# A vision block on one core: values per token tile through DRAM, masked key eviction, new attention banks, q/k/v products nine tiles late, ternary rounding on POOL

## What is computed

```python
x = patches(img)                       # 64 x 36 x 768
x = layernorm(x, ln1_g, ln1_b) @ W + bias
x = layernorm(x, ln2_g, ln2_b) + pe
h = concatenate(cls_token + cls_pos_embedding, x)          # 64 x 37 x 256
q, k, v = split_heads(layernorm(h) @ Wqkv + bqkv)          # 16 heads of 16
q, k = q * cos + rotate_half(q) * sin, k * cos + rotate_half(k) * sin
h = h + (softmax(q @ k.T / 4) @ v) @ Wout + bout
y = layernorm(h)
h = h + bitlinear(gelu(bitlinear(y, W1, b1)), W2, b2)      # weights rounded to -1, 0, 1 times mean |W|
```

## Time and profile before

| what | us |
| --- | --- |
| median of three runs | 387.02 (383.44 to 388.23) |
| the profiled execution | 389.49 |
| its span, first to last instruction | 387.7 |
| TensorE busy | 328.3 (85%) |
| VectorE busy | 276.0 (71%) |
| ScalarE busy | 219.3 (57%) |
| POOL busy | 160.4 (41%) |

### The profile page before, as it was taken

One profiled execution on the slowest core, in us unless ns is written; L12 is line 12 of the kernel. 1 busy time (PEld: TensorE's weight loads), 2 busy tenths in 40 slices (PEclk: granted clock), 3 DMA queues, 4 the chain that ended last, 5 costly groups with the idle time before them and its releaser, 6 DMA issues.

```text
span 387.7 us, 9782 instructions
## 1 busy us (share of the span) xinstructions
PE 328.3 (85%) x3548; PEld 255.5 (66%) x3548; DVE 276.0 (71%) x680; ACT 219.3 (57%) x398; POOL 160.4 (41%) x329
## 2 busy tenths in 40 slices
PE   0648999999999957699889898989886789999874
PEld 0436777777777632588778787878774467777553
DVE  1184577686776675447776767677766899999983
ACT  2344455545577312244555555555553799999993
POOL 4223265464654525324332333323204556656630
PEclk9996999999999997657999999999999999999997
DMA  8997050000000000000000000000000000100101
GB/s 225 311 399 225 9 210 1 2 2 2 0 2 1 0 2 0 2 1 3 2 0 0 0 0 0 0 0 0 0 2 1 1 2 27 43 27 30 43 28 61
DMA packets 9018, 16.10 MB, mean 42 GB/s; under 512 B 944, under 2 KB 5744, under 8 KB 8992
## 3 DMA queue, kind: packets, MB, share of 16 engines
q1 hardware_dynamic: 7936, 13.59, 10.3%
q10 hardware_dynamic: 1056, 2.18, 2.2%
HBM read 13.34 MB, written 2.42 MB: 41 GB/s over the span
## 4 chain that ended last, share of the span: by engine, by line
PE 54%; DVE 18%; ACT 12%; issue 9%; DMA 3%; POOL 3%; ACTq 0%; DVEq 0%; POOLq 0%
PE ps L331 13%; PE ps L407 9%; PE ps L357 7%; DVE sc L811 6%; PE ps L439 4%; DVE ximg L830 4%; PE ps L321 3%; DMA qkT<-in_W 3%; PE ps L415 3%; ACT ximg L1023 2%; PE ps L426 2%; ACT ximg L976 2%; PE ps L314 2%; PE ps L365 2%; PE ps L401 2%
## 5 line engine op out<-in xcount | busy, mean ns | idle before, releaser
L1057 POOL TENSOR_TENSOR rs<-rs,nhalf 128x1 f32<-128x1 f32 (+1 forms) x76 | 41.8, 557 | 120.4 <-DVE rs L622 50.8
L962 ACT ACTIVATE ximg<-ps,byp 128x222 f32<-128x222 f32 x64 | 25.0, 442 | 61.0 <-PE ps L447 54.0
L331 PE MATMUL ps<-w_in,xT 128*128 128x256 f32 (+1 forms) x228 | 55.3, 394 | 2.9 <-ACT xT L896 2.9
L331 PEld LDWEIGHTS ps<-w_in,xT 128*128 128x128 f32 (+1 forms) x228 | 42.8, 195 | 10.5 <-ACT xT L896 4.2
L407 PE MATMUL ps<-hnT,w_v 128*128 (+1 forms) x256 | 38.9, 300 | 12.7 <-ACT ximg L976 7.6
L1101 POOL TENSOR_TENSOR ximg<-qkT,ones_c 128x148 f32<-128x148 f32 x32 | 15.9, 497 | 80.7 <-PE ps L401 79.5
L407 PEld LDWEIGHTS ps<-hnT,w_v 128*128 128x128 f32 x256 | 34.2, 208 | 18.1 <-issue 16.9
L756 DVE TENSOR_TENSOR ximg<-ps,tab 111x512 f32<-111x512 f32 x32 | 22.1, 691 | 31.9 <-PE ps L426 31.9
L357 PE MATMUL ps<-w_qk,hnT 128*128 128x512 f32 (+1 forms) x76 | 37.9, 623 | 6.7 <-DVE qb L673 6.7
L896 ACT ACTIVATE xT<-ps 128x768 f32<-128x768 f32 (+1 forms) x19 | 15.1, 794 | 32.0 <-PE ps L321 32.0
L665 DVE TENSOR_TENSOR qa<-ps,tab 128x512 f32<-128x512 f32 (+1 forms) x19 | 13.1, 689 | 27.8 <-PE ps L314 27.8
(11 more groups left out here) (107 smaller groups left out, 770.5 us busy)
## 6 DMA issues: line engine op xcount, KB each, us to landing
ximg<-in_x SPq DMA_DIRECT2D x18, 384.0 KB, 15.8
out<-ximg SPq DMA_DIRECT2D x18, 128.0 KB, 1.7
ximg<-in_W SPq DMA_DIRECT2D x2, 1024.0 KB, 6.3
wide<-in_rows ACTq DMA_DIRECT2D x1, 768.0 KB, 15.1
w_qk<-in_Wqk SPq DMA_DIRECT2D x1, 512.0 KB, 15.0
qkT<-in_offsets ACTq DMA_DIRECT2D x1, 448.0 KB, 13.3
qkT<-in_W SPq DMA_DIRECT2D x1, 384.0 KB, 6.3
qkT<-in_W ACTq DMA_DIRECT2D x1, 384.0 KB, 11.3
```

Source lines behind the costliest of these rows:

```text
L331: pe.matmul(dst[0:n, :], xT[t % 2][:, k, 0:n], w_in[:, k, :], start=(k == 0), stop=False)
L962: ins = act.activation(vds[u][:, m, :, :].rearrange("p i (r t) -> p i r t", r=3), src, ACT.Identity, bias=b_v[:, m:m + 1])
L1057: pool.tensor_tensor(rs[u][0:n, i:i + 1], rs[u][0:n, i:i + 1], nhalf[0:n, :], ALU.pow).then_inc(S[done], 1)
```

## The change

1. The q/k product of a tile is done nine steps behind its pixels instead of four (`LAG = 9`), with VectorE's rotation, POOL's add and the transposes moved with it. `hnT` becomes a ring of seven tiles. The patch stage is 30 steps long on TensorE instead of 25.
2. A values product per token tile (`value_product`, two products of 256 columns) follows each q/k product. ScalarE evicts it by head parity with a column of ones per head, SP stores it in DRAM (`vsc`), and two loads a pair, 48 rows x 2 images x 544 bytes each, bring it back in block form; four buffers `vb`, cleared by POOL, take them. The per-pair values product, its eviction, its four transposes and VectorE's placing are gone.
3. The keys are evicted twice, each with a parity mask as scale, so `scores` reads `qkT` directly and POOL's staging is gone.
4. Probabilities are padded to 64 columns a head and turned two heads at a time, four transposes in each of banks 4 and 5; `attend` is 16 products of 34 columns (32 records) into banks 6 and 7 by turns; the output is turned into the ends of banks 4 and 5. The attention loop is written out.
5. The values' bias goes through Wo into the output's offset row (`out_offset`), which needs Wo at the start; Wo and Wv are loaded after pixel tiles 2 and 3.
6. The six ternary passes go to POOL, after its last patch step; the two absolute sums of ScalarE go to steps 10 and 12, the total and the scales to steps 15 and 16.

```diff
+LAG = 9
+HB = LAG - 2
...
+            sp.dma_start(w_o[:], a["Wo"].rearrange("(k p) n -> p k n", p=128)).then_inc(S["ld_o"], 16)
+            load_x(3)
+            sp.dma_start(w_v[:], a["Wv"].rearrange("(k p) n -> p k n", p=128)).then_inc(S["ld_v"], 16)
...
+            def load_values(p):
+
+                if p < 4:
+                    sp.wait_ge(S["v_zero"], p + 1)
+                else:
+                    sp.wait_ge(S["o_ready"], p - 3)
+                for e in range(2):
+                    src = bass.AP(vsc.tensor, PW * p * VROW + e * HC * VW,
+                                  [[VROW, 48], [TOK * VROW, 2], [1, HC * VW]])
+                    sp.dma_start(vb[p % 4][64 * e:64 * e + 48, :, e, :], src).then_inc(S[f"vb{p % 4}"], 16)
...
+            for t in range(NT):
+                store_values(t)
+            sp.wait_ge(S["v_stored0"], 16 * (NT // 2))
+            sp.wait_ge(S["v_stored1"], 16 * (NT // 2))
+            for p in range(4):
+                load_values(p)
+            store_values(NT)
+            sp.wait_ge(S["v_stored0"], 16 * (NT // 2 + 1))
+            for p in range(4, NP):
+                load_values(p)
...
             def patch_step(s):
                 if live(s - 2, NT + 1):
                     position_rows(s - 2)
-                if live(s - 6, NT + 1):
-                    turn_qk(s - 6)
+                if live(s - LAG - 2, NT + 1):
+                    turn_qk(s - LAG - 2)
...
-                if live(s - 4, NT + 1):
-                    qk_product(s - 4)
+                if live(s - LAG, NT + 1):
+                    qk_product(s - LAG)
+                    value_product(s - LAG)
                 if live(s - 3, NT + 1):
                     turn_h(s - 3)
+                if s == 0:
+                    out_offset()
...
+            def turn_out(p, b):
+
+                pe.wait_ge(S["o_norm"], p + 1)
+                pe.wait_ge(S[f"p_evac{b}"], min(p + 2, NP))
+                war(pe, "o_canvas4" if b == 4 else "o_canvas", p, 1)
+                m = b - 4
+                pe.transpose(ps[:, b, O_AT:O_AT + SPAN], at[p % 4][0:SPAN, 128 * m:128 * m + 128],
+                             ident[0:SPAN, 0:SPAN]).then_inc(S[f"o_turned{b}"], 1)
...
+            def attention_step(s):
+                if live(s, NP):
+                    scores(s)
+                if live(s - 3, NP):
+                    turn_out(s - 3, 5)
+                    turn_out(s - 3, 4)
+                if live(s - 2, NP):
+                    attend(s - 2)
                 if live(s - 1, NP):
+                    turn_probs(s - 1, 4)
+                    turn_probs(s - 1, 5)
...
+            pe.wait_ge(S["y_mid"], NT + 1)
+            attention_step(0)
+            patch_step(NT + LAG + 1)
+            pe.wait_ge(S["h_ready"], NT + 1)
+            pe.wait_ge(S["v_evac"], NT + 1)
+            attention_step(1)
+            patch_step(NT + LAG + 2)
             pe.wait_ge(S["a_init"], 2)
+            for s in range(2, NP + 1):
+                attention_step(s)
...
+            v.wait_ge(S["orow"], 1)
+            v.tensor_tensor(qko[:, 2 * D:3 * D], ps[0:K3, 7, 0:D], qko[:, 2 * D:3 * D], ALU.add).then_inc(S["bmix"], 1)
             v.wait_ge(S["b_hi"], 2)
             leave_out(bres[0:K3, qo], bhi[0:K3, qo], 0, qko).then_inc(S["b_res"], 1)
...
+            v.wait_ge(S["p_zero"], 1)
+            attention_step(0)
+            patch_step(NT + LAG + 1)
+            v.wait_ge(S["qk_rot"], NT + 1)
+            v.memset(ps[:, 6, 0:NH * VW], 1.0).then_inc(S["a_init"], 1)
+            attention_step(1)
+            v.wait_ge(S["qk_canvas"], NT + 1)
+            v.memset(ps[:, 7, 0:NH * VW], 1.0).then_inc(S["a_init"], 1)
...
-            act.wait_ge(S["ld_offs"], 32)
+            act.wait_ge(S["bmix"], 6)
             act.activation(bhi[0:K3, qo], qko, ACT.Copy).then_inc(S["b_hi"], 1)
...
+            def attended_out(p, b):
+                act.wait_ge(S[f"o_turned{b}"], p + 1)
+                act.wait_ge(S[f"p_turned{b}"], min(p + 3, NP))
+                at0 = PW * p
+                act.activation(qkT[:, b - 4, at0:at0 + PW].rearrange("p (i t) -> p i t", i=2), ps_aT(b), ACT.Copy
+                               ).then_inc(S["o_canvas4" if b == 4 else "o_canvas"], 1)
...
+            def attention_step(s):
+                if live(s - 3, NP):
+                    attended_out(s - 3, 4)
+                    attended_out(s - 3, 5)
+                if live(s - 1, NP):
+                    probs_out(s - 1, 4)
+                    probs_out(s - 1, 5)
                 if live(s, NP):
+                    exponentials(s)
...
+            ternary(0, w1, w1t)
+            ternary(1, w2, w2t)
```

More of the change, by code:

```diff
@@ L216, in vit_block @@
         ymid = two("ymid", [128, D])
+        hnT = [sb(f"hnT{u}", [128, 2, 128]) for u in range(HB)]
+        vt = two("vt", [128, 2, HC, VW])
         hn = two("hn", [128, D])
@@ L219, in vit_block @@
         qb = two("qb", [128, 2 * D])
-        qr = two("qr", [128, 2 * D])
         def rows(t):
@@ L309, in _, with out_offset @@
             pe.wait_ge(S["ld_tab"], 16)
+            def out_offset():
+                pe.wait_ge(S["ld_o"], 16)
+                for k in range(2):
+                    mm = pe.matmul(ps[0:K3, 7, 0:D], bass.AP(byp, 2 * KP + k, [[2 * KP + 2, 128], [0, K3]]),
+                                   w_o[:, k, :], start=(k == 0), stop=(k == 1))
+                mm.then_inc(S["orow"], 1)
             def add_rows(dst, t, which, only=False):
@@ L339, in position_rows, with value_product @@
                 add_rows(ps_pos[0:rows(t), :], t, PE_ROWS, only=True).then_inc(S["pos_ready"], 1)
+            def value_product(t):
+                pe.wait_ge(S["h_canvas"], min(t + HB - 1, NT + 1))
+                war(pe, "v_evac", t, 1)
+                if t == 0:
+                    pe.wait_ge(S["ld_v"], 16)
+                n = rows(t)
+                for k in range(2):
+                    mm = pe.matmul(ps_v[0:n, :], hnT[t % HB][:, k, 0:n], w_v[:, k, :], start=(k == 0), stop=(k == 1))
+                mm.then_inc(S["v_ready"], 1)
             def turn_h(t):
@@ new lines, in scores, with turn_probs @@
+                            dst = ps[64 * i:64 * i + TOK, r, 2 * TOK * c:2 * TOK * c + 2 * TOK]
+                            mm = pe.matmul(dst.rearrange("p (e t) -> p e t", e=2),
+                                           qkT[32 * r:32 * r + 32, c, at0:at0 + TOK], rhs, start=True, stop=True)
+                mm.then_inc(S["s_ready"], 1)
+            def turn_probs(p, b):
+                pe.wait_ge(S["s_exp"], p + 1)
+                war(pe, f"p_evac{b}", p, 1)
+                for g in range(4):
+                    at0 = 2 * 64 * (4 * (b - 4) + g)
+                    flat = pr[p % 2][0:SPAN, :, :].rearrange("p h t -> p (h t)")
+                    mm = pe.transpose(ps[0:SPAN, b, SPAN * g:SPAN * g + SPAN], flat[:, at0:at0 + SPAN],
+                                      ident[0:SPAN, 0:SPAN])
+                mm.then_inc(S[f"p_turned{b}"], 1)
@@ new lines, in turn_out, with attend @@
+            def turn_out(p, b):
[5 more added lines that the diff above has]
+                             ident[0:SPAN, 0:SPAN]).then_inc(S[f"o_turned{b}"], 1)
+            def attend(p):
+                pe.wait_ge(S["p_evac4"], p + 1)
+                pe.wait_ge(S["p_evac5"], p + 1)
+                pe.wait_ge(S[f"vb{p % 4}"], 32 * (p // 4 + 1))
+                war(pe, "o_norm", p)
+                for g in range(HC):
@@ L784, in _ @@
-            steps(v, attention_step, A_FIRST, A_LAST, NP + 2, begin=5)
+                    soften(s)
+            v.wait_ge(S["p_zero"], 1)
[6 more added lines that the diff above has]
+            v.memset(ps[:, 7, 0:NH * VW], 1.0).then_inc(S["a_init"], 1)
+            for s in range(2, NP + 3):
+                attention_step(s)
```

398 lines of the change are left out of this document (154 added, 244 removed).

## The result

| | before | after |
|---|---|---|
| median | 385.43 us (4 runs) | 409.85 us (4 runs) |
| lowest and highest | 383.44 and 388.23 | 408.62 and 411.06 |
| span of the profiled execution | 387.7 us | 407.9 us |
| mean granted clock of TensorE, of 2.4 GHz | 0.95 | 0.82 |
| one pair of images in attention | 3.91 us | 4.39 us |

The changed kernel takes 1.063 times as long as the kernel before, with a 95% interval of 1.054 to 1.071. The forecast was 378.3 us in a range of 366 to 396, with 0.20 for a slower kernel. The result lies outside the range, near the 415 of rival C. The 0.95 of the kernel before is that of the profiled execution; in its 21 executions run beside the variants it is 0.945 to 0.966, with times of 384 to 390 us.

A forecast was written before the change was run, and what follows sets the result against it. TensorE's work and waits were taken to bound up to the first output product, forecast at 277.7; with 94.7 carried over 372.4, plus 6.5 for the clock, span 378.9, 8.8 below 387.7; from median 387.02, 378.3 us, range 366 to 396.

The forecast's parts named there:

- rival C: Attention: the clock stays low through it, as the work is sparser; all 93 us of it give 415; chance 0.13.
- The clock: From the hand-over, about 175 us: TensorE at 1.2 GHz for 20 us, costing 6.5 us.
- Start: Before tile 1's statistics: an added VectorE add and ScalarE's copy cost 1.4 us; bounds 0, or 4 if Wo is late.
- Nine tiles late: Patch stage: steps without q/k 4.53 us, full ones 6.93, lone q/k 3.74; putting q/k off wins nothing; ends at 170.2.
- Hand-over: Between patch stage and attention: 6.3 us from pair 0's scores, third attention step at 176.5; values' DRAM trip hidden.
- Rival E: Attention: the values aren't there and attend waits on its two loads; 22 us in all, about 400; chance 0.08.
- Attention at the high clock: Attention loop: 3.2 us a pair, set by ScalarE's evictions, output transposes, attend and probability transposes; ends 2.9 and 3.6.
- Rival D: Attention: the eviction loop or attend is dearer, 3.6 to 3.9 a pair adding 11 to 20: 389 to 398; chance 0.14.
- the 372.4 forecast for a high clock: Whole span before the clock's cost: first output product at 277.7 against 292.96, the rest of 94.7 us carried over.
- A: Whole kernel: the forecast as reckoned, with 20 us at the low clock, 374 to 384; chance 0.45.
- B: Attention: the clock comes back within 7 us, or attend records scale with columns: 363 to 373; chance 0.20.

The follow-up runs named there:

- the burst: The changed kernel with sixteen dense fp32 products of 128x240 put once into attention's step 10, hand-over left unfilled: 390.96 us, one execution.
- the transposes: The changed kernel with four 101x101 transposes put into each attention step behind its scores, hand-over left unfilled: 422.8 us, one execution.
- LAG = 5: The changed kernel with q/k and values products five tiles late instead of nine, and POOL's clearing of the probabilities' padding moved ahead: 407.12 us, one execution.
- the filled version: The changed kernel with seven unused fp32 products of 128x240 on TensorE in the hand-over's three waits: 368.74 us, ratio 0.953 to the kernel before.

## Why the prediction failed, point by point

**The clock: the step that failed.** The prediction says "I expect it at 1.2 GHz for as long as last time, 20 us", and takes 6.5 us for it. It had the place right (the hand-over; 173 against "from about 175") and the cause (TensorE working in pieces). The length was taken from the earlier trace rows, where the clock had come back amid another kind of work. That is the step that failed: the length of the low stretch was carried over to a stage that no longer had that work. Measured: 143 us, to 3.6 us behind the start of the first output product. A pair lost 4.39 - 3.06 = 1.33, and over some 31 steps that is 41, the distance between the spans of 407.9 and 366.5. The prediction had both halves of the argument in hand under rival C: "The work is sparser than now (no 128-row products", and 20 us needed even with them; it gave that 0.13. What it had against it, "at 2.4 GHz it held for 107 us at 88% busy", speaks only of keeping the clock, and the burst and the transposes show that work which kept it did not win it back. Which part of the removed work had brought it back in the kernel before is not shown. The price per microsecond was right: 10 us at the low clock cost 1.33 / 4.39 x 10 = 3.0, forecast 3.3.

On the pages: the Trainium skill (TensorE: Matmul & The Clock Gate, "What's actually happening") says that activity releases the throttle, soon after sustained work begins. By that the time would have been near 373. The trace disagrees where the activity is small products and transposes: 102.58 us busy of the 112 from 186 to 298 did not release it. It agrees for dense ones, in the burst. The same page of the Trainium skill ("HAM oscillation — how this bites in real kernels") tells of a kernel whose clock falls while it waits for transfers; here the waits were on other engines, and pieces of 1.33 and 0.81 us stood ahead of the fall. The warning of the Trainium skill of a monitor that stayed throttled (same page, "Seeing it yourself") was the better guide, but stuck is not what the runs show: the low state was left 4.5 us behind the start of the burst, and behind the output products in every kernel.

**Start: both terms right, and the landing of the weights not seen.** Chain of waits, before and after:

```profile
1.65 11.32 DMA qkT<-in_W
...
21.78 0.75 DVE pos_rows L630
...
23.45 1.02 DVE st L563 x2
```

```profile
1.64 9.59 DMA qkT<-in_W
...
19.92 0.75 DVE pos_rows L670
20.67 0.34 DVE qkT L695
...
21.04 0.85 ACT qkT L976
...
22.85 1.02 DVE st L603 x2
```

From the rounding of the position rows to tile 1's statistics it is 23.45 - 21.78 = 1.67 before and 22.85 - 19.92 = 2.93 after: the added VectorE operation and the copy, 0.34 and 0.85 on the path, cost 1.26, forecast 1.4. But the first weights landed 9.59 us after issue in place of 11.32, and the position rows' rounding starts 1.9 earlier; that is most of the 2.6 between the 42.9 forecast for tile 3's product and the 40.34 measured. The kernels of this study that differ only far behind the start had 8.89 to 11.86 for the same load, so I give the difference no cause; absolute times in two profiled executions can differ by 1 or 2 us by it. Wo landed at 18.5, and the one product that waited 1.5 for it is not on the chain.

**Nine tiles late: right.** Steps without q/k 4.53 as forecast, full ones 6.94 for 6.93, lone products 3.65 for 3.74 from tile 14 on (the step from tile 11 to 12 takes 4.34, so that the seven take the 26.2 forecast). Scores of the first pair start at 168.26 for 170.2: tile 8 was 2.5 early by the start, and the full steps gave 0.5 of that back. LAG = 5 confirms that putting q/k off costs, 1.2 to 1.3 us a tile.

**Hand-over: right.** The third attention step starts at 175.08, 6.8 us behind the first scores; 6.3 forecast. TensorE is idle for 3.6 of them, about 4 forecast. Between the last store and attend nothing waits on a transfer: the 64 loads land in 1.9 at the median, and POOL's ternary passes take 1.97, 1.90 and 1.89 each, six of them from 173 to 185, a third of the 32 us that one row of another form had bounded. Rival E had nothing to it.

**Attention at the high clock: right, with a size off by 4%.** 3.06 us a pair for 3.2; ScalarE's second eviction releases the output transposes, as said:

```profile
PE ps L484 <- ACT ximg L1009: 14.3, 23, 0.6
```

```profile
PE ps L484 <- ACT ximg L1000: 5.8, 16, 0.4
```

These are waits of TensorE from 186 to 256 (us in total, times, longest): first the filled version, 0.62 us a pair, then the changed kernel, 0.36 a pair, where TensorE's own work is longer. The term that was mis-sized is attend: 0.72 for its 32 records, not the 0.98 forecast. The forecast scaled the 0.74 of the earlier trace rows by the number of records. But of those 24 only 20 have 51 columns and 4 have 17 (the order of before shows them as 10 and 2 products), 1,088 columns in all, and 32 x 34 is 1,088 too: the same columns took the same time. By them the forecast's loop would have been 2.96, near its lower end of 2.9, and 3.06 was measured. At the low clock the same loop takes 4.39, forecast 4.7. Rival D did not occur.

With these the sum nearly closes for the kernel with the filled hand-over. Of the 372.4 forecast for a high clock, 0.7 goes because its third step starts at 175.78 and not at 176.5, and 31 x 0.14 = 4.3 for the loop and the two turns behind it: 367.4, and its span is 366.5. The 0.9 left lies at the end of attention. The 0.7 is what the weights' earlier landing left after the full steps and the hand-over had each taken about 0.5 more than forecast: luck, not foresight.

**The chances.** 0.47 for faster rested on a clock that comes back, in all of A and B. For how long it might stay low (6 us in B, 20 in A, all of attention in C), the trace of before shows one case of 6 us, ended amid lone q/k products, and one of 20, ended amid pairs with a values product; the changed attention has neither. That was reason to hold C at least as likely as B. A small slip beside it: half of C's 0.13 is 0.07 and not the 0.08 that stands in the sum for slower, which changes nothing.

## What to carry to other kernels

A change that empties a stage of TensorE's large products may leave it unable to win back its clock, however busy it stays: so ask of each stage both whether it starts with the high clock and whether its own work could restore it, and do not carry over the length of a low stretch from a stage with other work. Where the clock falls in short waits between two stages, a little work without a use in those waits can be the cheapest edit: here seven products for 41 us. Fill all of them; the middle one of three alone gave nothing. Align two profiles at a common event before a difference in absolute times is read as an effect: the first load alone moved everything by up to 3 us here. And a busy share that rises after a change, as here from 88% to 92%, can be the sign of a slower clock and not of better use.

## What was not expected of the hardware

- Keeping the clock and winning it back differ widely. Attention kept 1.00 with TensorE busy 55.68 of 70 us, and stayed at 0.50 with it busy 100.00 of 100 us, with the same work and more.
- What was done at the low clock mattered: it did not rise in over 100 us of 101x101 transposes and products of 37 weight columns, and rose within 5 us of 128x128 products by 240 columns in a row. One such product among the small ones in each step left it low for 99 us.
- A fall can follow on little. In the changed kernel it came behind idle pieces of 1.33 and 0.81 us within 3.8 us, and with three products of about 0.5 us, one in each gap, it did not come (one execution).
- POOL's pass over 2,048 columns took 1.9 us, also the one that writes bf16, while the pass of 2,368 columns to bf16, which reads one row of 37 columns 64 times over, had taken 6.2: the cast is not what made it dear, and a row of another form bounds little on that engine.
